# A cross-attention and mixture-of-experts kernel: four groups of expert tiles in place of three, two norms moved to VectorE, five result buffers

## The chip, the core and the metric

The kernel runs on one core of one Trainium2 chip. The metric is the device time of one execution in microseconds (us). Engines are called PE (TensorE), DVE (VectorE), ACT (ScalarE), POOL (GpSimd) and SP (SyncE, which here only issues DMAs). Each engine works through its own list of instructions in order; they meet at semaphores.

## What is computed

Two layers over 8 batches of 256 tokens of width 128. The part that the change touches is the end of the second layer:

```python
x = x + tanh(g_xattn[1]) * xattn(layernorm(x), ctx)      # 16 heads of width 8, softmax
z = layernorm(x)                                         # the fourth norm, per batch of 256 tokens
gates = z @ gate_w + gate_b                              # 8 experts
scores, idx = top_k(gates, 2); g = softmax(scores)
for each expert e: h = gelu(z @ w1[e] + b1[e]); y[e] = h @ w2[e] + b2[e]
x = x + tanh(g_ffn[1]) * (sum of the two chosen y, weighted by g)
```

Tokens, weights and results of this part are fp32.

## The kernel before, in words

**Tiles.** Every token is written twice, once for each chosen expert, into a DRAM table `sorted_rows`, at a row that groups the tokens by expert (`sort_rows(b)`: four indirect DMAs from GpSimd for each batch b). The expert layer then runs over NT = 23 tiles of 256 rows; each tile belongs to one expert. For tile n SP loads the expert's weights (`load_weights(n)`, 4 buffers) and the 256 rows (`load_rows(n)`, 4 buffers); PE transposes the rows (`turn_tokens`), DVE copies them out of the accumulation bank (`take_tokens`), PE makes the hidden layer (`hidden`), ACT the GELU (`gelu_tile`), PE the result (`output`), DVE adds the bias into a result buffer (`weigh`, buffer n % 3) and GpSimd scatters it (`scatter`, two indirect DMAs). At the end all results are read back and added.

**Groups.** Which expert a tile has depends on how many tokens chose each expert, so tiles are planned in groups (`PHASES`): after batch 5 the first 5 tiles are certain to be full, after batch 6 two more, and after batch 7 the remaining 16. `begin_tiles(phase)` is that planning: a chain of 17 small DVE instructions, each waiting for the one before it. It ends by setting the tile's expert and place, which SP reads into a register before it issues a load.

**Slots.** The attention over batch n is `step_c(n)`, written out as 18 slots, k = 0 to 17, and every engine runs its own list for each slot. In step n the attention of batch n runs beside the scores of batch n + 1 (`m`) and the end of batch n - 1 (`o`): softmax sums are turned, inverted and spread (slots 2 to 5), the heads are scaled (`on`, slot 4), multiplied by We (slot 8), added to x (slot 8, line 1222), its variance is taken (slots 10, 11), GpSimd makes the reciprocal deviation (`rstd_of`, lines 496 and 499) and the norm (`fourth_norm`, lines 585 to 594), PE turns the normed tokens (slot 16, line 1700). The gates of batch n - 2 are made in slot 0, its two experts picked (`top_two`, `choose`), and its rows placed (`find_place`, slot 13, line 1291).

Step 8 is the tail: no attention is left in it, only the end of batch 7, the gates and places of batch 6, and the first tiles. PE's list there is: gates of batch 6 (slot 0), turn the sums (2), rank the choices of batch 6 (3), spread the inverted sums (5), We (8), then tile 0 and tile 1 (`turn_tokens(0)`, `hidden(0)`, `turn_tokens(1)`, `hidden(1)`, slot 10), then the normed tokens of batch 7 (16). DVE takes the tokens of tiles 0 and 1 in slot 12 and then runs `begin_tiles(1)`. SP issues the first weight load only when all attention is done (`attended`), because weight and row buffers lie on memory that attention uses, and the first row load when batches 0 to 5 are sorted. GpSimd's list in step 8 is: norm of batch 7, then `sort_rows(6)`.

After step 8 a loop over n runs `hidden(n + 1)`, `turn_tokens(n + 2)`, `output(n)` on PE and `take_tokens(n + 2)`, `weigh(n)` on DVE; the gates, choice and place of batch 7 and `begin_tiles(2)` sit inside the first two passes.

Of the kernel before, what the change touches and what calls it, by code (L numbers as in the profile page):

```python
# [16 lines left out]
U32 = mybir.dt.uint32  # L17
# [5 lines left out]
P = 128  # L23
# [20 lines left out]
PHASES = ((0, 5), (5, 2), (7, NT - 7))  # L44
KNOWN = (BATCH - 3, BATCH - 2, BATCH - 1)
# [84 lines left out]
def flamingo(nc, t):  # L130
    ctx = ExitStack()
    with ctx:
# [150 lines left out]
        nmax = [sb(f"nmax{i}", [P, 2, 2, 2, QUADS], scope=c) for i in range(2)]  # L283
        c.close()
# [4 lines left out]
        soft = sb("soft", [P, 4, TILES], scope=d)  # L289
        weight = sb("weight", [P, TILES, 2], scope=d)  # L290
        spare = [sb(f"spare{i}", [P, 2], scope=d) for i in range(2)]
        to_row = [sb(f"to_row{i}", [P, 2], U32, d) for i in range(4)]
        wbuf = [sb(f"wbuf{i}", [P, PACK], scope=d) for i in range(WB)]
        xg = [sb(f"xg{i}", [P, 2, ROW], scope=d) for i in range(4)]
        xg_t = [sb(f"xg_t{i}", [P, SLOT], scope=d) for i in range(2)]
        hid = [sb(f"hid{i}", [P, HC, SLOT], scope=d) for i in range(2)]
        yout = [sb(f"yout{i}", [P, SLOT], scope=d) for i in range(3)]
# [42 lines left out]
        def _(sp):  # L340
# [117 lines left out]
            for i in range(3):  # L458
                sp.wait_ge(sem(f"y_out{i}"), 32 * ((NT - 1 - i) // 3 + 1))
# [15 lines left out]
        def _(pool):  # L475
# [104 lines left out]


# [61 lines left out]
            for n in range(1, BATCH + 1):  # L643
                if n + 1 < BATCH:
                    widen_v(Step(0, n + 1, BATCH))
                if 2 <= n < BATCH:
                    choose(pool, n - 2)
                fourth_norm(Step(0, n - 1, BATCH))
                if n >= 2:
                    sort_rows(n - 2)  # L650

            def scatter(n):
# [3 lines left out]
                for i in range(2):  # L656
                    pool.indirect_dma_start(  # L657
                        out=y_rows[:, :], out_offset=bass.IndirectOffsetOnAxis(ap=to_row[n % 4][:, i:i + 1], axis=0),
                        in_=yout[n % 3][:, i * P:(i + 1) * P], in_offset=None)\
                        .then_inc(sem(f"y_out{n % 3}"), 16)  # L660
# [1135 lines left out]
```

## Time and profile before

| what | value |
|---|---|
| median of 3 runs | 412.39 us (411.47 to 415.35) |
| profiled execution, own time | 412.65 us |
| its span in the profile | 410.9 us |
| PE busy | 307.9 us (75%) |
| DVE busy | 265.3 us (65%) |
| ACT busy | 198.1 us (48%) |
| POOL busy | 162.6 us (40%) |

The span is what the trace shows of that execution; 1.75 us of its time lie outside it. All times below are microseconds from the start of the span. The attention steps run until about 280, step 8 and the first tiles from 280 to 311, the rest of the tiles until 384, and the final sums until the end. Busy time is an average over stages with different limits, so what counts is the stage in which a change lies.

### The profile page before, as it was taken

What the parts mean: (1) busy time and instruction counts of PE and PEld (TensorE: products, weight loads), DVE (VectorE), ACT (ScalarE), POOL (GpSimd) and SP (SyncE); (2) the same over time, 40 slices, a digit from 0 to 9 for tenths busy, and PEclk for the clock granted to TensorE, in tenths of its full rate; (3) what the DMA queues carried; (4) which work ended last, traced back from release to release, by engine and by line L of the source; (5) the groups of instructions that cost most, each with busy time, mean ns of one, the idle gap of its engine ahead of it and who ended that gap; (6) DMA issues with size and microseconds to landing.
All of it is one profiled execution on the core that took longest, in us unless ns stands there. A gap on an engine that the chain in (4) does not pass through costs nothing.

```text
span 410.9 us, 7400 instructions
## 1 busy us (share of the span) xinstructions
PE 307.9 (75%) x2316; PEld 250.3 (61%) x2317; DVE 265.3 (65%) x878; ACT 198.1 (48%) x395; POOL 162.6 (40%) x289
## 2 busy tenths in 40 slices
PE   1568785271476999999999999995498999999300
PEld 0457774210333787877877787664398999999300
DVE  4647887498983978978979797855274323232162
ACT  1136664454923667666566666563153544454100
POOL 4350111450552401215272644633627644554432
PEclk9959999575557799999999999998699999999855
DMA  7434672554010111101110111005536878874171
GB/s 196 150 128 180 241 274 46 69 86 109 1 38 2 24 32 24 25 22 46 37 46 21 49 27 40 21 8 172 178 101 203 259 227 246 233 219 137 47 247 51
DMA packets 30618, 43.76 MB, mean 106 GB/s; under 512 B 5075, under 2 KB 24086, under 8 KB 30198
## 3 DMA queue, kind: packets, MB, share of 16 engines
q1 hardware_dynamic: 25798, 35.71, 30.1%
q0 software_dynamic: 3008, 6.23, 4.8%
q10 hardware_dynamic: 1776, 1.38, 1.1%
q8 instruction: 18, 0.29, 0.3%
q14 instruction: 18, 0.15, 0.1%
HBM read 21.99 MB, written 15.01 MB: 90 GB/s over the span
## 4 chain that ended last, share of the span: by engine, by line
PE 63%; DVE 11%; DMA 8%; issue 7%; POOL 6%; ACT 2%; DVEq 0%; SPq 0%; POOLq 0%
PE bank L1419 57%; DMA k_all<-k_hi 3%; DVE x L1390 2%; POOL k_all L315 2%; DVE nmax L1172 1%; PE bank L1734 1%; DMA xg<-sorted_rows 1%; DMA y_in<-y_rows 1%; DVE xn L919 1%; DMA sorted_rows<-token_row,place 1%; PE bank L1667 1%; POOL x L547 1%; PE bank L1445 1%; DMA x<-in_x 1%; PE bank L1679 1%
## 5 line engine op out<-in xcount | busy, mean ns | idle before, releaser
L837 ACT ACTIVATE probs<-bank 128x512 f32<-128x512 f32 x128 | 71.0, 597 | 43.9 <-PE bank L1419 43.7
L1172 DVE TENSOR_REDUCE nmax<-bank 128x2 f32<-128x512 f32 x128 | 81.7, 678 | 4.4 <-PE bank L1419 3.7
L848 ACT ACTIVATE hid<-bank,wbuf 128x256 f32<-128x256 f32 x92 | 39.6, 475 | 52.7 <-PE bank L1419 52.7
L657 POOL DMA_INDIRECT y_rows<-yout,to_row x46 | 44.0, 957 | 39.3 <-DVE yout L1379 31.4
L1419 PE MATMUL bank<-q_st,k_quad 128*128 128x256 f32 x256 | 56.0, 308 | 0.8 <-ACT probs L837 0.7
L1419 PE MATMUL bank<-k_quad,q_st 128*128 128x256 f32 x256 | 53.7, 296 | 1.6 <-ACT q_st L800 0.7
L1419 PE MATMUL bank<-xg_t,wbuf 128*128 128x256 f32 x184 | 45.3, 390 | 2.4 <-issue 1.8
L1419 PEld LDWEIGHTS bank<-q_st,k_quad 128*128 128x128 f32 x256 | 38.7, 193 | 11.9 <-ACT probs L837 11.2
L1419 PE MATMUL bank<-wbuf,hid 128*128 128x128 f32 x368 | 45.0, 275 | 0.5 <-DVE yout L1379 0.5
L1419 PEld LDWEIGHTS bank<-wbuf,hid 128*128 128x128 f32 x368 | 43.0, 192 | 0.8 <-DVE yout L1379 0.7
L1419 PEld LDWEIGHTS bank<-k_quad,q_st 128*128 128x128 f32 x256 | 40.5, 196 | 3.9 <-DVE nmax L1172 2.2
L496 POOL TENSOR_TENSOR var_eps<-mv,eps_row 128x2 f32<-128x2 f32 (+1 forms) x20 | 4.0, 201 | 90.2 <-DVE mv L934 87.4
L1419 PEld LDWEIGHTS bank<-xg_t,wbuf 128*128 128x128 f32 x184 | 34.2, 196 | 7.0 <-issue 3.1
L606 POOL DMA_INDIRECT sorted_rows<-token_row,place x32 | 31.7, 991 | 11.1 <-issue 8.6
L1419 PE MATMUL bank<-probs,v_st 128*32 128x256 f32 x512 | 34.3, 385 | 0.7 <-ACT probs L837 0.7
L1363 DVE COPY xg_t<-bank 128x256 f32<-128x256 f32 x23 | 9.8, 424 | 32.9 <-PE bank L1734 32.8
L1379 DVE TENSOR_TENSOR yout<-bank,wbuf 128x256 f32<-128x256 f32 x23 | 9.7, 424 | 20.2 <-PE bank L1419 20.2
L1419 PEld LDWEIGHTS bank<-probs,v_st 128*32 128x32 f32 x512 | 13.4, 109 | 10.6 <-ACT probs L837 1.0
L1445 PE MATMUL bank<-ident,ctx_in 128*128 128x128 f32 x16 | 3.9, 331 | 20.7 <-DVE xn L946 12.2
L575 POOL TENSOR_TENSOR v_st<-v,bv 128x64 f32<-128x64 f32 x32 | 9.2, 323 | 23.0 <-PE bank L1419 22.8
L1192 DVE TENSOR_TENSOR q_st<-bank,q_st 128x512 fp32r<-128x512 f32 x16 | 11.0, 685 | 9.8 <-PE bank L1419 9.8
L499 POOL TENSOR_TENSOR rstd<-var_eps,half_neg 128x2 f32<-128x2 f32 (+1 forms) x20 | 15.8, 788 | 1.6
(237 smaller groups left out, 589.4 us busy)
## 6 DMA issues: line engine op xcount, KB each, us to landing
wbuf<-in_moe_pack SPq DMA_DIRECT2D x23, 578.0 KB, 4.1
sorted_rows<-zeros SPq DMA_DIRECT2D x15, 572.0 KB, 4.1
k_quad<-k_all SPq DMA_DIRECT2D x64, 48.0 KB
xg<-sorted_rows SPq DMA_DIRECT2D x23, 132.0 KB, 3.5
ctx_in<-in_ctx SPq DMA_DIRECT2D x8, 128.0 KB, 2.8
x<-in_x SPq DMA_DIRECT2D x4, 256.0 KB, 5.1
k_all<-k_hi SPq DMA_DIRECT2D x16, 64.0 KB
k_all<-k_lo SPq DMA_DIRECT2D x16, 64.0 KB
```

The source lines that it names most:

```text
L315: eng.dma_start(k_all[32 * j + 8 * s:32 * j + 8 * s + 8, g, :].bitcast(F32), src[r0:r0 + 8, :].bitcast(F32)).then_inc(sem(f"k_slotted{s // ...
L499: pool.tensor_tensor(out[:, 0:tiles], eps_sum[:, 0:tiles], half_neg[:, 0:tiles], ALU.pow)\
L575: pool.tensor_tensor(dst[:, :, :, 48 * r:48 * r + 8], heads(v1f[:, ds(s.n * SEQ + i * P, P)]), heads(bv1[:, :]), ALU.add)\
L606: pool.indirect_dma_start(out=sorted_rows[:, :], out_offset=bass.IndirectOffsetOnAxis(ap=place[:, c:c + 1], axis=0), in_=token_row[b % 3][ ...
L657: pool.indirect_dma_start(out=y_rows[:, :], out_offset=bass.IndirectOffsetOnAxis(ap=to_row[n % 4][:, i:i + 1], axis=0), in_=yout[n % 3][:, ...
L837: act.activation(probs[quad % 2][:, j, :, :], bank[2 + j % 2][:, :] .rearrange("p (r s) -> p r s", r=2), ACT.Exp, scale=SC1)\
L848: act.activation(hid[n % 2][:, ch, :], bank[ch][:, 0:SLOT], ACT.Gelu, bias=wbuf[n % WB][:, B1P + ch:B1P + ch + 1]).then_inc(sem("gelued"), 1)
L1172: dve.tensor_reduce(nmax[m.par][:, gp, qt, :, j], bank[QUERY_BANKS[u % 3]][:, :].rearrange("p (r s) -> p r s", r=2), AX.X, ALU.max, negate ...
L1192: dve.tensor_tensor(qs, bank[5][:, :].rearrange("p (g s) -> p g s", g=2), qs.bitcast(F32), ALU.add).then_inc(sem("q_shifted"), 1)
L1363: dve.tensor_copy(xg_t[n % 2][:, :], bank[6][:, 0:SLOT]).then_inc(sem("xg_t_ready"), 1)
L1379: dve.tensor_tensor(yout[n % 3][:, :].rearrange("p (i d) -> p i d", d=DM), bank[5][:, 0:SLOT].rearrange("p (i d) -> p i d", d=DM), wbuf[n ...
L1419: return pe.matmul(out, lhsT, rhs, start=start, stop=stop, **kw)
```

## The change

- The groups are now (0, 3), (3, 2), (5, 2), (7, 16): the first three tiles are planned after batch 4, in step 7 slot 6, the next two after batch 5 (step 7 slot 14), two more after batch 6 (step 8 slot 12).
- Weight and row buffers, scatter indices and shares are moved to memory that attention does not use; SP no longer waits for `attended`.
- PE's list in step 8: gates of batch 6 (slot 0, another bank), `turn_tokens(0)` (1), sums (2), ranks of batch 6 (3), `hidden(0)` and `turn_tokens(1)` (4), spread (5), We (8), `hidden(1)`, `turn_tokens(2)` and `output(0)` (10), normed tokens of batch 7 (16).
- DVE's list in step 8: gates and choice of batch 6 (0), reciprocal (1), `take_tokens(0)` (2), `on` (4), place of batch 6 (5), x (8), variance and the new `late_norm(7)` (10, 11), then `take_tokens(1)`, `take_tokens(2)`, `weigh(0)` and `begin_tiles(2)` (12).
- The norms of batches 6 and 7 are made by DVE (`late_norm`, four instructions), GpSimd only makes the reciprocal deviation. In step 8 GpSimd runs `sort_rows(6)` first and that of batch 7 second.
- Five result buffers in place of three, seven sets of scatter indices in place of four.

```diff
+YB = 5
+PHASES = ((0, 3), (3, 2), (5, 2), (7, NT - 7))
+KNOWN = (BATCH - 4, BATCH - 3, BATCH - 2, BATCH - 1)
...
-            sp.wait_ge(sem("attended"), 4 * BATCH)
+            first = PHASES[1][0]
             sp.wait_ge(sem("tiles_set"), 2)
-            for n in range(WB):
+            for n in range(first):
                 load_weights(n)
-            for i in range(2):
-                sp.wait_ge(sem(f"rows_sorted{i}"), 64 * 3)
-            for n in range(4):
+            sp.wait_ge(sem("rows_sorted0"), 64 * 3)
+            sp.wait_ge(sem("rows_sorted1"), 64 * 2)
+            for n in range(first):
                 load_rows(n)
-            for n in range(4, NT):
+            for n in range(first, NT):
                 if n == PHASES[1][0]:
                     sp.wait_ge(sem("tiles_set"), 4)
-                    sp.wait_ge(sem("rows_sorted2"), 64)
+                    sp.wait_ge(sem("rows_sorted1"), 64 * 3)
                 if n == PHASES[2][0]:
                     sp.wait_ge(sem("tiles_set"), 6)
+                    sp.wait_ge(sem("rows_sorted2"), 64)
+                if n == PHASES[3][0]:
+                    sp.wait_ge(sem("tiles_set"), 8)
...
+                if b.n >= BATCH - 2:
+                    pool.wait_ge(sem(f"rows_sorted{(b.n - 3) % 2}"), 64 * ((b.n - 3) // 2 + 1))
+                    pool.tensor_copy(token_row[b.n % 3][:, :, :, DM], row_no[:, 2 * b.n:2 * b.n + 2, :])\
+                        .then_inc(sem("rows_named"), 1)
+                    rstd_of(b.n + (LN4 + 1), mv[b.par], var_eps[b.par], rstd[b.par], 2)
+                    return
...
-                pool.wait_ge(sem("rows_named"), 2 * b + 2)
+                late = max(0, b - (BATCH - 3))
+                pool.wait_ge(sem("rows_named"), 2 * b + 2 - late)
+                if late:
+                    pool.wait_ge(sem("xn4_copied"), late)
...
+                if n == BATCH:
+                    sort_rows(n - 2)
                 fourth_norm(Step(0, n - 1, BATCH))
-                if n >= 2:
+                if 2 <= n < BATCH:
...
+                    if is_step(s, BATCH) and k == 5:
+                        gelu_tile(0)
                     if is_step(s, BATCH) and k == 15:
-                        gelu_tile(0)
+                        gelu_tile(1)
...
+                        if is_step(o, BATCH - 2) or is_step(o, BATCH - 1):
+                            late_norm(o.n)
...
+                    if is_step(s, BATCH - 1) and k == 6:
+                        begin_tiles(0)
                     if is_step(s, BATCH - 1) and k == 14:
-                        begin_tiles(0)
+                        begin_tiles(1)
+                    if is_step(s, BATCH) and k == 2:
+                        take_tokens(0)
                     if is_step(s, BATCH) and k == 12:
-                        take_tokens(0)
                         take_tokens(1)
-                        begin_tiles(1)
+                        take_tokens(2)
+                        weigh(0)
+                        begin_tiles(2)
                     if m.valid and k == 9:
                         split_maxima(m, 0)
                     if m.valid and k == 13:
                         shift_q(m, 0)
                     if m.valid and 0 <= k - QUERY_LAG < 16:
                         maximum(k - QUERY_LAG)
+
+            def late_norm(b):
+
+                late = b - (BATCH - 3)
+                dve.wait_ge(sem("rstd_done"), b + (LN4 + 1))
+                dve.wait_ge(sem("rows_named"), 2 * b + 2 - late)
+                for k, ready in ((0, "xn4_ready"), (1, "xn4_copied")):
+                    for i in range(2):
+                        ins = norm(token_row[b % 3][:, i, k, 0:DM], x[:, b * SEQ + i * P:b * SEQ + (i + 1) * P], b % 2, i)
+                    ins.then_inc(sem(ready), 1)
...
-                if n >= 3:
-                    dve.wait_ge(sem(f"y_out{n % 3}"), 32 * (n // 3))
-                dve.tensor_tensor(yout[n % 3][:, :].rearrange("p (i d) -> p i d", d=DM),
+                if n >= YB:
+                    dve.wait_ge(sem(f"y_out{n % YB}"), 32 * (n // YB))
...
-            for n in range(NT):
+            add_gate_bias(BATCH - 1, bank[4][:, 0:16])
+            top_two(BATCH - 1)
+            choose(dve, BATCH - 1)
+            dve.tensor_tensor(soft[:, 0, :], top[:, :, 1], top[:, :, 0], ALU.subtract).then_inc(sem("top_gap"), 1)
+            for n in range(1, NT):
                 if n + 2 < NT:
                     take_tokens(n + 2)
                 weigh(n)
-                if n == 0:
-                    add_gate_bias(BATCH - 1, bank[4][:, 0:16])
-                    top_two(BATCH - 1)
-                    choose(dve, BATCH - 1)
-                    dve.tensor_tensor(soft[:, 0, :], top[:, :, 1], top[:, :, 0], ALU.subtract).then_inc(sem("top_gap"), 1)
                 if n == 1:
                     find_place(BATCH - 1, bank[4][:, 16:40])
-                    begin_tiles(2)
+                    begin_tiles(3)
...
+                        pe.wait_ge(sem("q_shifted"), 2 * BATCH)
+                        project_gates(BATCH - 2, bank[5][:, 0:16])
+                    if is_step(s, BATCH) and k == 1:
                         pe.wait_ge(sem("s_maxed"), 16 * BATCH)
-                        project_gates(BATCH - 2, bank[0][:, 0:16])
+                        turn_tokens(0)
                     if is_step(s, BATCH) and k == 3:
-                        rank_choices(BATCH - 2, bank[1])
+                        pe.wait_ge(sem("gates_ready"), BATCH - 1)
+                        rank_choices(BATCH - 2, bank[5][:, 16:40])
+                    if is_step(s, BATCH) and k == 4:
+                        pe.wait_ge(sem("exped"), 16 * BATCH)
+                        hidden(0)
+                        turn_tokens(1)
                     if s.valid and s.n >= 2 and k == 11:
                         pe.wait_ge(sem("x3_done"), o.n + 1)
                         rank_choices(s.n - 2, bank[7])
                     if is_step(s, BATCH) and k == 10:
+                        hidden(1)
+                        turn_tokens(2)
                         pe.wait_ge(sem("rank_step"), 3 * (BATCH - 2) + 2)
-                        pe.wait_ge(sem("counted"), 2)
-                        pe.wait_ge(sem("exped"), 16 * BATCH)
-                        pe.wait_ge(sem("q_shifted"), 2 * BATCH)
-                        turn_tokens(0)
-                        hidden(0)
-                        turn_tokens(1)
-                        hidden(1)
+                        pe.wait_ge(sem("counted"), 3)
+                        output(0)
...
-                if n and n + 1 < NT:
+            for n in range(1, NT):
+                if n + 1 < NT:
                     hidden(n + 1)
+                if n == 1:
+                    project_gates(BATCH - 1, bank[4][:, 0:16])
                 if n + 2 < NT:
                     turn_tokens(n + 2)
                 output(n)
-                if n == 0:
-                    project_gates(BATCH - 1, bank[4][:, 0:16])
                 if n == 1:
                     rank_choices(BATCH - 1, bank[4][:, 16:40])
```

## Rows read from the trace of the kernel before

**Rows 1.** Stretches: PE, PEld, DVE, ACT, POOL busy us (count); granted clock; DMA share
```profile
285.00:286.00 1.00, 0.77 (x5) 0.77 (x6) 0.71 (x6) 0.24 (x2) 0.00 (x0) 0.78 0.98 351
330.00:360.00 30.00, 30.00 (x210) 27.95 (x209) 8.61 (x32) 13.86 (x33) 15.31 (x16) 1.00 0.78 233
```

**Rows 2.** The chain of work that ended last: start, length, what
```profile
286.64 4.96 DMA xg<-sorted_rows
...
310.58 1.97 PE bank L1419 x8
```

**Rows 3.** Timeline of DVE, step 7: start, length, engine, line, operation, out<-in, count
```profile
270.01 0.69 DVE L1216 TENSOR_TENSOR on<-av,bank 128x512 f32<-128x512 f32 x1 [0.75 <-PE bank L1679]
...
272.90 0.48 DVE L1222 SCALAR_TENSOR_TENSOR x<-bank,tg,x 128x256 f32<-128x256 f32 x1 [2.21 <-PE bank L1419]
...
275.81 0.22 DVE L1316 TENSOR_SCALAR whole<-count 128x8 f32<-128x8 f32 x1
...
279.90 0.16 DVE L1355 TENSOR_TENSOR used<-base,ends 128x8 f32<-128x8 f32 x1
```

**Rows 4.** First weight loads (timeline, SP), and landing of row loads (line 434)
```profile
281.26 3.76 SPq L425 DMA_DIRECT2D wbuf<-in_moe_pack  x4
...
DMA to landing us min/median/max: 2.9/3.5/5.0
```

**Rows 5.** Timeline of DVE and PE in step 8
```profile
280.85 0.17 DVE L1250 TENSOR_TENSOR gates<-bank,gate_b 128x16 f32<-128x16 f32 x1 [0.80 <-PE bank L1419]
...
282.72 0.35 DVE L1210 RECIPROCAL sums_inv<-bank 128x32 f32<-128x32 f32 x1
...
283.79 0.66 PE L1679 MATMUL bank<-ident,inv_wide 128*128 128x128 f32 x4 [0.75 <-ACT inv_wide L812]
284.49 0.69 DVE L1216 TENSOR_TENSOR on<-av,bank 128x512 f32<-128x512 f32 x1 [1.41 <-PE bank L1679]
...
285.59 0.16 DVE L1291 SCALAR_TENSOR_TENSOR place<-top_f,rank 128x4 uint32<-128x4 f32 x1
```

**Rows 6.** Timeline of GpSimd: end of batch 7, then the sort of batch 6
```profile
288.44 0.19 POOL L496 TENSOR_TENSOR var_eps<-mv,eps_row 128x2 f32<-128x2 f32 x1 [6.25 <-DVE mv L934]
288.71 0.73 POOL L499 TENSOR_TENSOR rstd<-var_eps,half_neg 128x2 f32<-128x2 f32 x1
...
291.49 1.08 POOL L606 DMA_INDIRECT sorted_rows<-token_row,place  x1 [0.18 <-issue]
...
295.39 0.95 POOL L606 DMA_INDIRECT sorted_rows<-token_row,place  x1 [0.30 <-issue]
```

**Rows 7.** Timeline of DVE: four norms of 128x128 in the third norm
```profile
112.61 1.10 DVE L919 TENSOR_SCALAR xn<-x,mv,rstd 128x128 f32<-128x128 f32 x4
```

**Rows 8.** Timeline of PE: hidden(0), hidden(1), output(0)
```profile
293.00 3.34 PE L1419 MATMUL bank<-xg_t,wbuf 128*128 128x256 f32 x8 [0.61 <-DVE xg_t L1363]
...
297.13 1.97 PE L1419 MATMUL bank<-xg_t,wbuf 128*128 128x256 f32 x8 [0.56 <-issue]
...
299.37 1.95 PE L1419 MATMUL bank<-wbuf,hid 128*128 128x128 f32 x16
```

**Rows 9.** Timeline of DVE among the first tiles
```profile
297.21 0.17 DVE L1316 TENSOR_SCALAR whole<-count 128x8 f32<-128x8 f32 x1
...
300.12 0.16 DVE L1355 TENSOR_TENSOR used<-base,ends 128x8 f32<-128x8 f32 x1
...
301.35 0.42 DVE L1379 TENSOR_TENSOR yout<-bank,wbuf 128x256 f32<-128x256 f32 x1 [0.35 <-PE bank L1419]
...
306.45 0.17 DVE L1316 TENSOR_SCALAR whole<-count 128x8 f32<-128x8 f32 x1
...
310.05 0.42 DVE L1363 COPY xg_t<-bank 128x256 f32<-128x256 f32 x1
```

**Rows 10.** Result buffers (yout): who waited for their instructions (us, times)
```profile
  DVE to_row L1370: 7.8, 8
...
  PE bank L1419: 0.5, 1
```

More of the change, by code:

```diff
@@ L283, in flamingo @@
         nmax = [sb(f"nmax{i}", [P, 2, 2, 2, QUADS], scope=c) for i in range(2)]
+        soft = sb("soft", [P, 4, TILES], scope=c)
+        weight = sb("weight", [P, TILES, 2], scope=c)
+        spare = [sb(f"spare{i}", [P, 2], scope=c) for i in range(2)]
+        to_row = [sb(f"to_row{i}", [P, 2], U32, c) for i in range(YB + 2)]
+        wbuf = [sb(f"wbuf{i}", [P, PACK], scope=c) for i in range(WB)]
+        xg = [sb(f"xg{i}", [P, 2, ROW], scope=c) for i in range(4)]
         c.close()
@@ L288, in flamingo @@
         d = ctx
[L289 to L294, printed above, removed]
         xg_t = [sb(f"xg_t{i}", [P, SLOT], scope=d) for i in range(2)]
         hid = [sb(f"hid{i}", [P, HC, SLOT], scope=d) for i in range(2)]
-        yout = [sb(f"yout{i}", [P, SLOT], scope=d) for i in range(3)]
+        yout = [sb(f"yout{i}", [P, SLOT], scope=d) for i in range(YB)]
         y_in = [sb(f"y_in{i}", [P, BT, 2, DM], scope=d) for i in range(NBLK)]
@@ L456, in load_sums @@
                 sp.dma_start(y_in[k][:, :, :, :], y_tiles[:, BT * k:BT * k + BT, :, :]).then_inc(sem(f"y_landed{k}"), 16)
-            for i in range(3):
-                sp.wait_ge(sem(f"y_out{i}"), 32 * ((NT - 1 - i) // 3 + 1))
+            for i in range(YB):
+                sp.wait_ge(sem(f"y_out{i}"), 32 * ((NT - 1 - i) // YB + 1))
             load_sums(0)
@@ L657, in scatter @@
                     pool.indirect_dma_start(
-                        out=y_rows[:, :], out_offset=bass.IndirectOffsetOnAxis(ap=to_row[n % 4][:, i:i + 1], axis=0),
-                        in_=yout[n % 3][:, i * P:(i + 1) * P], in_offset=None)\
-                        .then_inc(sem(f"y_out{n % 3}"), 16)
+                        out=y_rows[:, :], out_offset=bass.IndirectOffsetOnAxis(ap=to_row[n % (YB + 2)][:, i:i + 1], axis=0),
+                        in_=yout[n % YB][:, i * P:(i + 1) * P], in_offset=None)\
+                        .then_inc(sem(f"y_out{n % YB}"), 16)
             for n in range(NT):
@@ L669, in add_last @@
                 k = NBLK - 1
-                pool.wait_ge(sem("v_step"), 49)
+                pool.wait_ge(sem("v_step"), 64)
                 pool.wait_ge(sem(f"y_landed{k}"), 16)
@@ L851, in _ @@
             unrolled(step_c, BATCH)
-            for n in range(1, NT):
+            for n in range(2, NT):
                 gelu_tile(n)
@@ L858, in load_sums @@
                 act.dma_start(y_in[k][:, :, :, :], y_tiles[:, BT * k:BT * k + BT, :, :]).then_inc(sem(f"y_landed{k}"), 16)
-            for i in range(3):
-                act.wait_ge(sem(f"y_out{i}"), 32 * ((NT - 1 - i) // 3 + 1))
+            for i in range(YB):
+                act.wait_ge(sem(f"y_out{i}"), 32 * ((NT - 1 - i) // YB + 1))
             load_sums(1)
@@ L1315, in begin_tiles @@
                 dve.wait_ge(sem("moe_set"), MOE_SET)
-                dve.tensor_scalar(whole[:, 0, :], count[:, phase, :], exact if phase == 2 else -exact, 1.0 / SLOT,
+                dve.tensor_scalar(whole[:, 0, :], count[:, phase, :], exact if phase == len(PHASES) - 1 else -exact, 1.0 / SLOT,
                                   ALU.add, ALU.mult).then_inc(sem("v_step"), 1)
@@ L1366, in take_tokens @@
                    .then_inc(sem("named"), 1)
-                if n >= 4:
-                    dve.wait_ge(sem(f"y_out{(n - 4) % 3}"), 32 * ((n - 4) // 3 + 1))
+                if n >= YB + 2:
+                    dve.wait_ge(sem(f"y_out{(n - YB - 2) % YB}"), 32 * ((n - YB - 2) // YB + 1))
                 dve.wait_ge(sem("named"), 2 * n + 1)
-                dve.scalar_tensor_tensor(to_row[n % 4][:, :], names, -1.0, spare[n % 2][:, :], ALU.add, ALU.add)\
+                dve.scalar_tensor_tensor(to_row[n % (YB + 2)][:, :], names, -1.0, spare[n % 2][:, :], ALU.add, ALU.add)\
                    .then_inc(sem("named"), 1)
@@ L1757, in _ @@
             unrolled(step_c, BATCH)
-            for n in range(NT):
-                if n and n + 1 < NT:
+            for n in range(1, NT):
+                if n + 1 < NT:
                     hidden(n + 1)
+                if n == 1:
+                    project_gates(BATCH - 1, bank[4][:, 0:16])
                 if n + 2 < NT:
```

19 lines of the change are left out of this document (9 added, 10 removed).

## The prediction, made before the changed kernel was run

> **What bounds the kernel now.** I read the chain of work that ended last first, then the stretches by engine, then the timeline around the end of attention. Late in the run PE is busy 30.00 of 30.00 us and its weight loads 27.95 [rows 1]: PE sets the pace there (210 matmuls in 30 us, 26 a tile: some 3.7 us a tile), and nothing that other engines do in that stretch shortens it. The chain says where that stretch begins: hidden(4) starts at 310.58 [rows 2] and from there on it is matmuls to the last tile. So the question for any change ahead of it is when hidden(4) starts. Its reason is on DVE: the copy for tile 4 is taken at 310.05, right after the planning of the last group, which began at 306.45 [rows 9].
>
> Between attention and hidden(4) there is a gap that the change aims at. SP issues its first weights at 281.26 [rows 4], the first rows follow at 286.64 and take 4.96 us [rows 2], and PE starts hidden(0) only at 293.00 [rows 8]. Meanwhile the end of batch 7 runs through DVE and PE [rows 5], then GpSimd makes its norm and sorts batch 6 [rows 6].
>
> **The change, part by part.**
>
> *Planning and loading earlier.* DVE reaches slot 6 of step 7 when `on` ends at 270.70 and waits there until 272.90 [rows 3], so 2.2 us of the planning of the first group are covered. A planning with few tiles takes 297.21 to 300.28, 3.07 us [rows 9]; the same list beside GpSimd's norm took 275.81 to 280.06, 4.25 us [rows 3]. GpSimd has no norm at that moment now, so I take 3.07: done at 273.8, and x of batch 6 is 1.1 us late. SP's first weight load came 1.2 us after the end of the planning that it needs (280.06 to 281.26), four issues take 3.76 us, some 1.1 each [rows 3, 4]. Three weight loads then go out from 275.0 and the first rows at 278.4. Their landing takes 2.9 to 5.0 us [rows 4]; nearest is the load of before that also queued behind fresh weights, 4.96 [rows 2]. Rows of tile 0 land at 283.4, at 281.3 by the lower bound.
>
> *DVE in step 7* also gets the norms of batch 6: four norms take 1.10 us [rows 7], behind a wait of 1.0 us for the reciprocal deviation (288.44 to 289.44) [rows 6]. With x 1.1 late, place of batch 5 and the second planning move back by 2.7 us and the latter ends near 281.6. The gates of batch 6, taken at 280.85 before [rows 5], start some 0.8 late; with 1.9 us from gates to reciprocal (280.85 to 282.72) [rows 5], the reciprocal can't start before 283.5. That is covered by the rows of tile 0, which are later still. Attention itself is not touched: PE needs the place of batch 5 only in slot 16.
>
> *Tile 0 inside the tail.* PE's list is in order, so turn_tokens(0) holds it until 283.4. Four transposes take 0.66 us [rows 5], two half that: sums turned at 284.5, reciprocal 0.35 [rows 5] and copy 0.42 [rows 9] with their handoffs: hidden(0) starts at 285.6, 7.4 us earlier than the 293.00 of before. So the front does what it is built for. But the granted clock fell in the stretch 285 to 286 (mean 0.78) after PE had been mostly waiting [rows 1], and hidden(0) took 3.34 us against 1.97 for hidden(1) [rows 8], the difference between the levels of 1.2 and 2.4 GHz. PE waits as much here, so I take 3.34. It then turns tile 1 (0.35) and only after that spreads the inverted sums of batch 7 (0.66): `on` starts at 290.1 in place of 284.49 [rows 5]. This is the price: **the end of batch 7 and the place of batch 6 both stand behind tile 0 in PE's list, 5.6 us late.**
>
> *The new order on GpSimd.* Place of batch 6 is 1.26 us after `on` (284.49 to 285.75) [rows 5]: 291.4. GpSimd now runs sort_rows(6) before the reciprocal deviation of batch 7. Four indirect DMAs take 291.49 to 296.34, 4.85 us [rows 6], so from 291.7 to 296.5; with the row names and 1.0 us for the deviation [rows 6] it is there at 297.7. Before, it was there at 289.44, and the norm on GpSimd took from there to the sort at 291.49, about 1.9 us [rows 6]; DVE's 1.10 saves 0.8 of that, on a path that has become 8 us longer.
>
> *What is queued behind the wait.* DVE waits for that deviation in slot 11 with everything behind it: take_tokens(1), take_tokens(2), weigh(0), begin_tiles(2). PE waits for take_tokens(1) with hidden(1), output(0) and the turn of batch 7. Norms until 298.9, copy 0.42 [rows 9], hidden(1) at 299.5 against 297.13 [rows 8]: **2.4 us later than before, though hidden(0) was 7.4 earlier.** PE has then stood still since We, near 291.5, so I price hidden(1) at the lower clock, 3.34. The Trainium skill (TensorE: Matmul & The Clock Gate, section HAM oscillation) says the same of a PE that waits for data between short bursts: each burst begins at the lower clock. By that rule the sum is the one given here, without it 2.7 us less; the two levels in rows 8 agree with it, but no row of before shows this gap.
>
> *From hidden(1) to hidden(4).* hidden(1) 3.34, turn 0.35, output(0) 1.95 [rows 8]: weigh(0) at 305.25, before 301.35 [rows 9], 3.9 later. Then DVE's list is longer than before by a planning, which stood beside tile 1 there (297.21) and stands behind weigh(0) now: weigh 0.42, planning 3.07, gates and choice of batch 7 2.1, tokens of tile 3 0.7, weigh(1) 0.4, place 0.6, last planning 3.6 (306.45 to 310.05) [rows 5, 9]. take_tokens(4) at 316.15 and hidden(4) 0.53 later, as before (310.05 to 310.58), at 316.7 [rows 2, 9]: **6.1 us late.** PE's own work of three tiles fits inside that. GpSimd's sort of batch 7 and the loads of tile 7 follow the same place and planning, and keep their distance to hidden(7).
>
> *Buffers.* DVE waited 7.8 us in 8 waits for scatters before it could write indices; PE waited 0.5 us in all for result buffers [rows 10]. PE covers the former, so five buffers and seven sets are worth 0 to 0.5; I take 0. If the cover were gone they could give 7.8. Moving buffers in memory costs no instruction.
>
> Sum, on the profiled execution (412.65, of which 410.9 are the span): 412.65 + 6.1 = 418.75. It is 0.26 above the median of the runs, so **418.5** is predicted. Bounds: rows landing in 2.9 us gain only 1.2 (the reciprocal's 283.5 then rules), both hidden layers at the upper clock gain 2.7: 414.6. Two plannings on the path at 4.25 in place of 3.07 cost 2.4: 421.
>
> **The rivals.**
> - *A shorter hold-up.* Either the clock stays up (-2.7: 415.8), or GpSimd's sort does not hold the deviation, whose spans are rough in the profile: the deviation then starts 3.95 us after `on` (284.49 to 288.44) [rows 5, 6], at 294.0 in place of 296.7, again 415.8. For it: PE is not quite idle ahead of hidden(0). Against it: the sort's four spans follow each other at 1.3 us, and before, too, hidden(0) came cold after a wait. 0.15.
> - *The other side: the buffers pay.* If the waits of 7.8 us for scatters [rows 10] lie on PE's path after all, hidden behind modelled ends of matmuls, taking them away gives 418.5 - 7.8 = 410.7, not slower. It decides from 6.1 of the 7.8 on. Against it: 30.00 of 30.00 [rows 1] and 0.5 us [rows 10]. 0.07.
> - *The front keeps its gain.* If tile 1 did not wait for the norm of batch 7, hidden(0)'s 7.4 us would move all that follows: 405. Against it stand the written order of DVE's list and of GpSimd's. 0.07.
> - *The loads come no earlier.* If rows of tile 0 land at 291.6 as before, turn_tokens(0) holds PE and the whole tail by 8.2 us more: 426.7. Against it: the planning needs only batch 4. 0.05.
>
> **How the numbers follow.** The forecast has 0.66, its own range is 414.6 to 421.5. The range 410 to 422.5 takes in the shorter hold-up and the buffers and leaves out the front's gain, the late loads and a little of each edge, under 2 in 10. A measurement of this kernel can tell about 1% from no change, so the borders are 408.3 and 416.5. Slower: most of the forecast (0.58), the late loads and some of the shorter hold-up, 0.67. Same: the rest of these two and most of the buffers' case, 0.23. Faster: 0.10.
>
> **What would show it.** Rows of tile 0 in by 283 to 284 and hidden(0) near 285.6 show the front right; a PE gap of some 7 us between We and hidden(1), with DVE waiting for line 499 in it and GpSimd in four indirect DMAs ahead of line 499, shows the hold-up; hidden(1) at 3.3 us shows the clock; hidden(4) near 316.7 shows the sum. I am wrong if hidden(1) starts before 297, or if tiles late in the run take less than 3.7 us.

## The result, and the profile after

The changed kernel takes 419.56 us (median of 20 runs, 416.39 to 421.94) against 413.27 us for the kernel before beside it (20 runs, 410.51 to 416.43): ratio 1.0149, 95% interval 1.0123 to 1.0176. It is slower, by some 6.2 us by the ratio. 418.5 was forecast. The profiled execution has a span of 419.0 us, against 410.9.

Two executions are compared here from one landmark, since they part long before the change. PE's last product for the gates of batch 6 (slot 0 of step 8, the end of attention) stands at 280.13 in the kernel before and at 281.61 after. Timeline of PE, the kernel before, then after: start, length, engine, line, operation, out<-in, size, count, idle time before it and its releaser.

```profile
128.50 1.13 PE L1419 MATMUL bank<-silu,wq 128*128 128x512 f32 x2 [0.69 <-ACT silu L788]
...
280.13 0.61 PE L1419 MATMUL bank<-gate_w,xt 128*128 128x8 f32 x4
...
291.73 0.66 PE L1734 MATMUL bank<-ident,xg 128*128 128x128 f32 x2 [4.71 <-DMA xg<-sorted_rows]
```
```profile
128.46 2.07 PE L1452 MATMUL bank<-silu,wq 128*128 128x512 f32 x2 [0.69 <-ACT silu L803]
...
281.61 0.61 PE L1452 MATMUL bank<-gate_w,xt 128*128 128x8 f32 x4
```

The two products at 128.5 are the same code and took 1.13 us in one execution and 2.07 in the other; the granted clock from 128 to 130 was 0.86 and 0.50, and its mean from 100 to 140 was 0.63 and 0.52. What PE does from here to the landmark is the same work, and other executions of the changed kernel's code up to there reach the landmark anywhere from 277.73 to 281.72 (see the last section). So the 1.48 us, of the 8.1 between the spans, is put down to PE's clock in the two executions and not to the change. From the landmark, call it G, the change is read. Chain of waits that ended last, after (start, length, what):

```profile
275.15 0.48 SPq L423
...
279.61 5.20 DMA xg<-sorted_rows
284.95 0.41 PE bank L1772 x2
...
286.74 3.75 PE bank L1452 x8
290.50 0.43 PE bank L1772 x2
290.92 0.87 PE bank L1717 x4
291.81 0.70 DVE on L1233
292.56 1.16 PE bank L1452 x8
293.71 7.13 issue
300.84 3.75 PE bank L1452 x8
...
317.28 1.15 issue
318.43 1.96 PE bank L1452 x8
```

The rows of tile 0 land 8.3 us earlier than before, counted from G (turn_tokens(0) at G + 3.34, before G + 11.60). hidden(0) starts at 286.74 and takes 3.75 us; its eight products take 1.97 at the upper clock [rows 8]. Then We ends at 293.7, and PE stands for 7.13 us ahead of hidden(1) at 300.84. hidden(4), where the stretch paced by PE begins [rows 1, 2], is at 318.43: G + 36.82 against G + 30.45. That is 6.37 us, and from hidden(4) to the end of the span both take the same, 100.6 and 100.3 us.

What DVE and GpSimd did in the gap of 7.13 us (timelines, after):

```profile
291.81 0.69 DVE L1233 TENSOR_TENSOR on<-av,bank 128x512 f32<-128x512 f32 x1 [4.96 <-PE bank L1717]
...
292.92 0.16 DVE L1325 SCALAR_TENSOR_TENSOR place<-top_f,rank 128x4 uint32<-128x4 f32 x1
...
294.90 0.15 DVE L951 BATCH_NORM_AGGREGATE mv<-stats 128x2 f32<-128x6 f32 x1
299.29 1.12 DVE L936 TENSOR_SCALAR token_row<-x,mv,rstd 128x128 f32<-128x128 f32 x4 [4.24 <-POOL rstd L503]
300.32 0.42 DVE L1397 COPY xg_t<-bank 128x256 f32<-128x256 f32 x1
```
```profile
293.36 0.96 POOL L619 DMA_INDIRECT sorted_rows<-token_row,place  x1 [8.91 <-DVE place L1325]
...
297.14 0.96 POOL L619 DMA_INDIRECT sorted_rows<-token_row,place  x1 [0.30 <-issue]
298.10 0.21 POOL L587 COPY token_row<-row_no 128x4 f32<-128x4 f32 x1
298.25 0.20 POOL L500 TENSOR_TENSOR var_eps<-mv,eps_row 128x2 f32<-128x2 f32 x1
298.53 0.72 POOL L503 TENSOR_TENSOR rstd<-var_eps,half_neg 128x2 f32<-128x2 f32 x1
```

GpSimd had waited 8.91 us for the place of batch 6 and began its four scatters at 293.36. The variance of batch 7 was ready at 295.05, in the middle of them, and GpSimd reached it only at 298.25. DVE waited 4.24 us for the result, and take_tokens(1), for which PE waited, stood behind DVE's norms.

The granted clock in that time (stretches of 2 us: busy us and count of PE, PEld, DVE, ACT, POOL; granted clock; DMA share; GB/s):

```profile
294.00:296.00 2.00, 0.00 (x0) 0.00 (x0) 0.96 (x7) 0.00 (x0) 1.39 (x3) 0.94 0.10 34
296.00:298.00 2.00, 0.00 (x0) 0.00 (x0) 0.00 (x0) 0.00 (x0) 1.70 (x2) 0.50 0.20 68
...
302.00:304.00 2.00, 2.00 (x7) 1.55 (x6) 0.00 (x0) 1.17 (x3) 0.00 (x0) 0.50 0.04 8
304.00:306.00 2.00, 2.00 (x10) 1.80 (x9) 0.65 (x3) 0.73 (x2) 0.00 (x0) 0.50 0.00 0
306.00:308.00 2.00, 2.00 (x17) 1.95 (x17) 0.59 (x3) 0.38 (x1) 0.00 (x0) 1.00 0.00 0
```

It falls to 0.50 (1.2 GHz) while PE stands, and is still there until 306, so hidden(1) takes 3.75 us.

### The profile page after: what moved, and what is told of

The parts are those of the page before. It is cut to its first block, busy times and chain, and to the rows that moved or that the text cites. A ratio compares the mean times of both kernels' runs of the same rounds, so it can differ in the third digit from the quotient of the medians.

```text
span 419.0 us, 7426 instructions
## 1 busy us (share of the span) xinstructions
PE 311.3 (74%) x2317; PEld 252.4 (60%) x2318; DVE 267.3 (64%) x904; ACT 198.4 (47%) x395; POOL 158.9 (38%) x283
## 4 chain that ended last, share of the span: by engine, by line
PE 60%; DVE 11%; issue 11%; DMA 7%; POOL 5%; ACT 2%; SPq 1%; DVEq 0%; POOLq 0%; ACTq 0%
PE bank L1452 54%; DMA k_all<-k_hi 3%; DVE nmax L1189 2%; POOL k_all L316 2%; DMA y_in<-y_rows 2%; PE bank L1772 1%; DMA xg<-sorted_rows 1%; PE bank L1705 1%; DVE xn L936 1%; PE bank L1717 1%; PE bank L1478 1%; POOL x L551 1%; DMA x<-in_x 1%; POOL y_in L690 1%; DVE h L1103 1%
## 5 line engine op out<-in xcount | busy, mean ns | idle before, releaser
L1452 PE MATMUL bank<-xg_t,wbuf 128*128 128x256 f32 x184 | 47.4, 404 | 9.3 <-issue 8.6
L1452 PEld LDWEIGHTS bank<-xg_t,wbuf 128*128 128x128 f32 x184 | 35.4, 203 | 14.1 <-issue 9.8
```

What stands on the lines that cost most here:

```text
L1452: return pe.matmul(out, lhsT, rhs, start=start, stop=stop, **kw)
```

## The experiments

Every kernel below is the changed kernel with the edit shown, and its ratio is to the kernel before on the same chip. The times from G are from the profiled execution of each; from hidden(4) to the end of the span all take 100.3 to 100.9 us, so the fifth column carries the difference. Among eight of these executions whose code is the same up to hidden(0) (after, e1 to e4b, e6 and e7), hidden(0) starts between G + 5.06 and G + 5.91. So differences of less than about 0.9 us in one column tell nothing by themselves.

| kernel | tile 0 turned | hidden(1) | weigh(0) | hidden(4) | ratio (95% interval) |
|---|---|---|---|---|---|
| before | G+11.60 | G+17.00 | G+21.22 | G+30.45 | 1 |
| after | 3.34 | 19.23 | 25.77 | 36.82 | 1.0149 (1.0123 to 1.0176) |
| e1_rstd_first | 3.50 | 16.03 | 21.70 | 33.02 | 1.0062 (1.0027 to 1.0096) |
| e2_take1_early | 3.39 | 12.74 | 19.23 | 30.31 | 0.9967 (0.9937 to 0.9996) |
| e3_three_buffers | 3.58 | 20.00 | 26.77 | 37.85 | 1.0107 (1.0061 to 1.0154) |
| e4_warm | 3.41 | 22.01 | 25.94 | 37.02 | 1.0137 (1.0092 to 1.0182) |
| e4b_warm14 | 3.71 | 19.98 | 23.91 | 34.97 | 1.0070 (1.0028 to 1.0111) |
| e5_loads_late | 9.68 | 25.35 | 31.16 | 42.22 | 1.0238 (1.0182 to 1.0293) |
| e6_place_early | 3.55 | 16.40 | 22.71 | 33.77 | 1.0045 (1.0002 to 1.0089) |
| e9_pool_norms | 3.73 | 13.75 | 17.76 | 29.75 | 1.0013 (0.9974 to 1.0052) |
| e7_all | 3.38 | 13.45 | 18.31 | 28.22 | 0.9898 (0.9838 to 0.9959) |
| e8_front | 4.19 | 10.87 | 14.88 | 24.79 | 0.9849 (0.9797 to 0.9902) |

**The scatter ahead of the last reciprocal deviation.** GpSimd makes rstd(7) first:

```diff
-                if n == BATCH:
-                    sort_rows(n - 2)
                 fourth_norm(Step(0, n - 1, BATCH))
-                if 2 <= n < BATCH:
+                if n >= 2:
```

> Changed kernel, but in step 8 GpSimd makes the reciprocal deviation of batch 7 ahead of sort_rows(6), as before the change. Theory (DVE waits for the deviation behind the sort, and tile 1 behind DVE): the variance of batch 7 is there at 295.05 in the changed kernel's trace, so the deviation comes at 296.1 in place of 299.25 and hidden(1) starts about 3.0 us earlier, near 297.8; all that follows moves with it: about 416.5 where the changed kernel has 419.56. Rival (the sort does not hold the deviation): no change. Rival (buffers or the late part rule): no change.

GpSimd in the timeline of e1_rstd_first now waits for the variance and makes the deviation ahead of the scatters:

```profile
291.19 0.19 POOL L500 TENSOR_TENSOR var_eps<-mv,eps_row 128x2 f32<-128x2 f32 x1 [10.39 <-DVE mv L949]
291.45 0.72 POOL L503 TENSOR_TENSOR rstd<-var_eps,half_neg 128x2 f32<-128x2 f32 x1
292.37 1.11 POOL L619 DMA_INDIRECT sorted_rows<-token_row,place  x1 [0.20 <-issue]
```

Measured 417.29 us; hidden(4) at G + 33.02, 3.8 us earlier than in the changed kernel; hidden(1) is 3.2 earlier and weigh(0) 4.1. The hold-up by the scatters is real and is more than half of the loss.

**The tokens behind the norm.** DVE takes the tokens of tile 1 before it waits for rstd(7):

```diff
                         find_place(BATCH - 2, bank[5][:, 16:40])
+                        take_tokens(1)
...
-                        take_tokens(1)
```

> Changed kernel, but DVE takes the tokens of tile 1 right after the place of batch 6, ahead of x and of the norm of batch 7. Theory: hidden(1) no longer stands behind the norm and starts when We is done, near 293.9, at the upper clock (1.97 in place of 3.75 us); take_tokens(2) and weigh(0) still stand behind the norm, so weigh(0) comes near 301.1 in place of 307.38: about 6 us gained, 413.4. Rival (the end hangs on batch 7's norm alone and not on tile 1): at most 1 us gained.

Measured 413.13 us. PE and DVE in the timelines of e2_take1_early:

```profile
291.04 2.08 PE L1452 MATMUL bank<-we_pad,on 128*128 128x128 f32 x8 [0.78 <-DVE on L1233]
292.91 2.83 PE L1452 MATMUL bank<-xg_t,wbuf 128*128 128x256 f32 x8
...
297.77 1.12 DVE L936 TENSOR_SCALAR token_row<-x,mv,rstd 128x128 f32<-128x128 f32 x4 [3.32 <-POOL rstd L503]
```

hidden(1) follows We at once (G + 12.74; it takes 2.83 us where 1.97 were expected), and the whole loss is gone, though GpSimd's order is that of the change and DVE still waits 3.3 us for rstd(7).

**The result buffers.** `YB = 3` in place of 5 (with it five sets of indices in place of seven):

> Changed kernel with three result buffers and five sets of scatter indices. Theory (PE covers the waits for scatters): no change, 419.6, within 0.5 us; DVE waits for scatters again, some 8 us in all. Rival (the buffers pay up to 7.8 us and hide a larger loss elsewhere): up to 427.

Measured 418.74 us. The interval of the ratio (1.0061 to 1.0154) takes in the changed kernel's 1.0149 and is far from a loss of 7.8 us against it. hidden(4) is 1.03 us later, but 0.78 of that is there at hidden(0), ahead of the first result buffer, and from hidden(4) to the end it is 100.43 us against 100.57. Five buffers are worth nothing that can be seen. DVE's wait of some 8 us for scatters, which was expected back, did not come: with five sets of indices, one more than the kernel before has, DVE never waits for one. So this run tests the buffers, and seven sets against five, but not the four sets of before; those 7.8 us of waits [rows 10] cost the kernel before nothing that shows, as it takes 100.3 us from hidden(4) to the end and the changed kernel 100.6.

**The clock.** PE is kept busy ahead of hidden(1) with products whose results nobody reads:

```diff
                     if is_step(s, BATCH) and k == 10:
+                        for _ in range(24):
+                            mm(bank[4][:, 0:SLOT], ident[:, :], causal[:, 0:SLOT])
                         hidden(1)
```

> Changed kernel with 24 extra products of 128x256 on PE between We and hidden(1), into a bank that nobody reads; they add nothing to the result and fill some 5.8 of the 7.1 us in which PE waits. Theory: hidden(1) starts at the same time but at the upper clock, 1.97 in place of 3.75 us, with the turn and output(0) behind it some 0.8 us shorter: 2.6 us gained in all, 417.0. Rival (the clock is no part of the loss, the path goes through DVE alone): no change.

Measured 420.12 us: no gain. The 24 products were mis-sized: 5.8 us was expected for them. Each is two matmuls in the trace, together they took 10.53 us, and hidden(1) came 2.8 us late (G + 22.01). But from hidden(1) to weigh(0) it took 3.93 us in place of 6.54. So the same with `range(14)`:

> The changed kernel with 14 products whose results nobody reads, put on TensorE between the gates' products of batch 7 (L1720's part We) and hidden(1). The run with 24 of them showed 0.434 us for one (10.53 us for 24), so 14 take about 6.1 us, from some 293.7 to 299.8 in the changed kernel's frame, and end ahead of hidden(1)'s data (300.84). Theory (the low clock behind the idle stretch adds 1.8 us to hidden(1) and 0.6 us to output(0)): hidden(1) starts where it did, its 8 products take 1.9 to 2.0 us in place of 3.75, the step from hidden(1) to weigh(0) takes 3.9 us in place of 6.54, and the time is 2.6 us less than the changed kernel's: ratio 1.0085 to the kernel before. Rival (VectorE's planning of group 2 behind weigh(0), not TensorE's clock, sets hidden(4)): weigh(0) earlier, hidden(4) and the time where they were, ratio 1.014.

Measured 416.9 us. Timeline of PE in e4b_warm14:

```profile
291.53 2.08 PE L1452 MATMUL bank<-we_pad,on 128*128 128x128 f32 x8 [0.78 <-DVE on L1233]
293.40 7.08 PE L1452 MATMUL bank<-causal,ident 128*128 128x256 f32 x28
300.32 1.89 PE L1452 MATMUL bank<-xg_t,wbuf 128*128 128x256 f32 x8
```

The 14 products took 7.08 us where 6.1 were expected, so hidden(1) is still 0.75 us later than in the changed kernel (0.37 of it is there when tile 0 is turned). Yet it takes 1.89 us, and from hidden(1) to hidden(4) it is 14.99 us in place of 17.59: 2.60 less. Useless work buys back 1.85 us net. The second part of the loss is the clock, a consequence of the gap. The granted clock of e4b_warm14 there:

```profile
296.00:298.00 2.00, 2.00 (x11) 1.76 (x10) 0.00 (x0) 0.00 (x0) 1.80 (x4) 1.00 0.20 68
```

**The loads.** SP waits for the end of attention again before its first weights:

```diff
+            sp.wait_ge(sem("attended"), 4 * BATCH)
             first = PHASES[1][0]
```

> The changed kernel with SyncE waiting, ahead of the first loads of the experts' weights, for the end of attention, as the kernel before did. Theory (the early loads are worth what they save in turn_tokens(0)): the weights are issued at about 282.7 in place of 276.15, the rows of group 0 land at about 291, hidden(0) comes some 6.2 us later than in the changed kernel and everything behind it by as much, less what planning group 2 and the place of batch 6 no longer cost because VectorE does them inside the wait: between 3 and 6.2 us more, ratio 1.022 to 1.030. Rival (the loads are hidden anyway, the hold-up by GpSimd's scatters and VectorE's late norms is the whole loss): hidden(1) and hidden(4) stay where they are, ratio 1.015.

Measured 423.02 us. Tile 0 is turned 6.3 us later, and hidden(4) is 5.40 us later. The chain of waits in e5_loads_late shows why hardly anything of it was covered:

```profile
282.33 4.95 DMA xg<-sorted_rows
...
295.96 7.13 issue
303.09 3.75 PE bank L1453 x8
```

The hold-up ahead of hidden(1) is 7.13 us here too: it hangs on `on` and the place of batch 6, which stand behind tile 0 in PE's list, and moves with it. The early loads do gain; the gain is smaller than what the new order loses.

**The place of batch 6.** It is found right behind take_tokens(0), ahead of the wait for the spread:

```diff
-                    if is_step(s, BATCH) and k == 5:
-                        find_place(BATCH - 2, bank[5][:, 16:40])
...
                     if is_step(s, BATCH) and k == 2:
                         take_tokens(0)
+                        find_place(BATCH - 2, bank[5][:, 16:40])
```

> The changed kernel with one piece of VectorE's order moved: the place of batch 6 is found right behind take_tokens(0), ahead of the gates' addition that waits for TensorE's spread, in place of behind it. Theory (the scatter of batch 6 holds up GpSimd's last rstd because the place comes late): the four scatters run from about 288 to 292.8, ahead of the last variance (295.05) rather than across it; rstd(7) follows the variance at once, the late norms start at about 296 in place of 299.3, hidden(1) at 297.5 in place of 300.84, and the time is 3 us less than the changed kernel's: ratio 1.007, as with the rstd made first. Rival (the hold-up is the scatters' own cost to VectorE or to the DMA queues, wherever they stand): no change, ratio 1.014.

Measured 416.31 us; hidden(4) 3.05 us earlier. The scatters run from 287.97 to 292.72, and GpSimd then waits 2.46 us for the variance. That agrees with e1_rstd_first by another way: scatters out of the road of rstd(7), before it or after it, give 3 to 4 us.

**The norms.** GpSimd makes them as before, with the change's order of its list (that is, the scatters first):

```diff
-                if b.n >= BATCH - 2:
...
-                    return
...
-                late = max(0, b - (BATCH - 3))
+                late = 0
...
-                        if is_step(o, BATCH - 2) or is_step(o, BATCH - 1):
-                            late_norm(o.n)
```

> The changed kernel with one part undone: GpSimd makes the norms of batches 6 and 7 again, as in the kernel before; loads, groups, planning and buffers are those of the change, and GpSimd still sends batch 6's rows out (293.36 to 298.10) ahead of its last rstd. Theory (the loss comes from putting VectorE's norms, which wait for that rstd, ahead of take_tokens(1) in VectorE's order): VectorE has no wait of 4.2 us any more, take_tokens(1) follows the last variance (295.05 in the changed kernel's frame), hidden(1) starts at about 295.6 in place of 300.84 and hidden(4) some 5.2 us earlier; GpSimd's norm is ready at about 300.6 (rstd to 299.25, then 0.60, 0.18 and half of 1.17 us as in the kernel before), in time for TensorE's turn behind output(0). The time is 5.2 us less than the changed kernel's: ratio 1.002. Rival (GpSimd's slower norms hold up the gates of batch 7 by as much as VectorE's did hidden(1)): ratio 1.012 or more.

Measured 413.39 us, no different from the kernel before. PE, DVE and GpSimd in the timelines of e9_pool_norms:

```profile
295.15 0.39 DVE L1389 COPY xg_t<-bank 128x256 f32<-128x256 f32 x1
...
295.64 1.97 PE L1444 MATMUL bank<-xg_t,wbuf 128*128 128x256 f32 x8 [1.74 <-issue]
...
300.68 0.44 PE L1730 MATMUL bank<-ident,token_row 128*128 128x128 f32 x2 [1.07 <-POOL token_row L598]
```
```profile
297.33 0.96 POOL L613 DMA_INDIRECT sorted_rows<-token_row,place  x1 [0.30 <-issue]
298.31 0.21 POOL L500 TENSOR_TENSOR var_eps<-mv,eps_row 128x2 f32<-128x2 f32 x1
298.60 0.73 POOL L503 TENSOR_TENSOR rstd<-var_eps,half_neg 128x2 f32<-128x2 f32 x1
```

GpSimd's deviation is as late as ever, and its norm is slower. Nobody but the turn of batch 7 waits for it, and that waits 1.07 us, behind output(0). PE's gap shrinks to 1.74 us and hidden(1) runs at the upper clock, so hidden(4) comes 7.07 us earlier: 5.48 by hidden(1), 2.53 between hidden(1) and weigh(0), and 0.94 lost again behind weigh(0). 5.2 were expected, without the clock.

**Both orders mended, and a faster kernel.** First DVE's list alone:

```diff
-                    if is_step(s, BATCH) and k == 5:
-                        find_place(BATCH - 2, bank[5][:, 16:40])
...
+                        if is_step(o, BATCH - 1):
+                            take_tokens(2)
                         if is_step(o, BATCH - 2) or is_step(o, BATCH - 1):
                             late_norm(o.n)
...
                     if is_step(s, BATCH) and k == 2:
                         take_tokens(0)
+                        find_place(BATCH - 2, bank[5][:, 16:40])
+                        begin_tiles(2)
+                    if is_step(s, BATCH) and k == 5:
+                        take_tokens(1)
                     if is_step(s, BATCH) and k == 12:
-                        take_tokens(1)
-                        take_tokens(2)
                         weigh(0)
-                        begin_tiles(2)
```

> The changed kernel with VectorE's order rearranged throughout step 8: the place of batch 6 and the plan of group 2 stand right behind take_tokens(0), where VectorE waited 4.9 us; take_tokens(1) behind the gates' addition; take_tokens(2) between the last variance and the two late norms; weigh(0) after them. Theory (the loss is the order of VectorE's and GpSimd's work round hidden(1), nothing else of the change): hidden(1) follows the gates' products at once (about 293), the late norms come before 298, hidden(4) at about 309 in place of 318.4, and the time is some 9.5 us less than the changed kernel's: about 410 us, ratio 0.992. Rival (another stage behind hidden(4), such as the results' way out, takes over once the front is short): hidden(4) at 309, the time less by under 6 us, ratio 0.998 or more.

Measured 410.44 us, 1.0% below the kernel before. hidden(4) is 8.60 us earlier than in the changed kernel: 5.78 by hidden(1), 1.68 between hidden(1) and weigh(0) (the clock, in part: hidden(1) still takes 2.82), 1.14 behind weigh(0), where the planning of group 2 no longer stands. That planning takes 3.07 us, but behind weigh(0) DVE now waits 1.87 us for the gates of batch 7:

```profile
300.49 0.17 DVE L1285 TENSOR_TENSOR gates<-bank,gate_b 128x16 f32<-128x16 f32 x1 [1.87 <-PE bank L1453]
```

Then PE's and GpSimd's lists too, shown against the changed kernel:

```diff
-                if n == BATCH:
-                    sort_rows(n - 2)
...
-                    if is_step(s, BATCH) and k == 1:
+                    if is_step(s, BATCH) and k == 6:
                         pe.wait_ge(sem("s_maxed"), 16 * BATCH)
                         turn_tokens(0)
...
-                    if is_step(s, BATCH) and k == 4:
+                    if is_step(s, BATCH) and k == 9:
                         pe.wait_ge(sem("exped"), 16 * BATCH)
                         hidden(0)
```

In DVE's list `take_tokens(0)` stands in slot 5 here, `find_place` behind the variance, and `take_tokens(1)`, `begin_tiles(2)`, `take_tokens(2)` ahead of weigh(0) in slot 12. So it differs from e7_all in all three lists: the place of batch 6 and the planning of group 2 are later than there.

> The rearranged kernel of the run before (e7_all), with two more moves: TensorE does the sums and the spread of batch 7 while it waits for group 0's rows, and the gates' products ahead of hidden(0), as the kernel before did; GpSimd makes rstd(7) ahead of batch 6's scatters, and VectorE finds batch 6's place behind the last variance and plans group 2 behind take_tokens(1). Theory (what is left ahead of hidden(4) is the order of work in step 8): from the last gates' product of attention to hidden(4) 25.5 us in place of 28.2 in e7_all and 36.8 in the changed kernel, the gates' addition 5 us earlier, hidden(1) 2 to 3 us earlier, the time 2 to 3 us less than e7_all's: ratio 0.983. Rival (the later scatter of batch 6 and the later plan make group 2's rows land after TensorE is ready for them, or TensorE's low clock takes the gain back): hidden(4) where e7_all has it, ratio 0.990.

Measured 407.98 us, 1.5% below the kernel before. Timeline of PE in e8_front:

```profile
281.60 0.66 PE L1703 MATMUL bank<-ident,av 128*128 128x128 f32 x4 [0.18 <-ACT av L820]
...
284.51 0.66 PE L1715 MATMUL bank<-ident,inv_wide 128*128 128x128 f32 x4 [0.75 <-ACT inv_wide L825]
285.00 0.38 PE L1770 MATMUL bank<-ident,xg 128*128 128x128 f32 x2
285.95 1.75 PE L1450 MATMUL bank<-we_pad,on 128*128 128x128 f32 x8 [0.56 <-DVE on L1231]
287.48 3.02 PE L1450 MATMUL bank<-xg_t,wbuf 128*128 128x256 f32 x8
...
291.68 1.97 PE L1450 MATMUL bank<-xg_t,wbuf 128*128 128x256 f32 x8 [0.96 <-issue]
```

The sums now lie in the wait for tile 0's rows, as they lay in the wait for the loads before the change, and the spread stands ahead of tile 0, which then waits for nothing. Tile 0 is turned 0.8 us later than in e7_all, hidden(1) comes 2.6 us earlier and hidden(4) 3.4. That is the worth of the three lists together; no run moves PE's list alone. The profiled spans, 408.6 and 406.0, and G (279.88 and 280.81) agree with that; the two intervals of the ratio overlap, so the step from e7_all to e8_front rests on the trace.

## Why the prediction was right, step by step

Counted in the frame of before (1.48 us taken off the trace of after).

- *The front.* Planning(0) done 273.8 forecast, 273.7 measured; first weights 275.0 and 274.7; rows issued 278.4 and 278.1; landing 4.96 and 5.20; hidden(0) 285.6 and 285.3. Right, also that nothing of attention moved.
- *The price in PE's list.* `on` at 290.1, measured 290.3; place of batch 6 at 291.4, measured 291.6. Right. What it costs alone isn't shown: e8_front, which takes it away, wins 3.4 us over e7_all, but with changes in the lists of DVE and GpSimd.
- *DVE in step 7.* Mis-sized, without effect: the second planning was to end at 281.6 and the gates of batch 6 to start 0.8 late. It ended at 280.8, and the gates started on time.
- *The hold-up.* Scatters 291.7 to 296.5, measured 291.9 to 296.6; rstd at 297.7, measured 297.8; norms until 298.9 and 298.9; hidden(1) at 299.5, measured 299.4, 2.23 us late against G. e1, e2, e6 and e9 each break one link of it. What the prediction didn't see is how little had to be broken: it is the link from DVE's norms to take_tokens(1) that matters most, as e2 gives back all of the loss with the scatters where they were. It priced their move to DVE as 0.8 us saved; the e9 run shows their place in DVE's list as 7.07 us lost.
- *The clock.* Mis-sized. hidden(1) 3.34 was forecast, by hidden(0) of before, and measured 3.75: the clock was low for all of it, and for the turn and most of output(0) behind it. From hidden(1) to weigh(0) 5.75 were forecast, 6.54 measured. The trace agrees with what the prediction weighed from the Trainium skill (TensorE: Matmul & The Clock Gate, section HAM oscillation), that work behind such a wait begins at the lower clock: with PE kept at work the 2.60 us came back.
- *From weigh(0) to hidden(4).* 11.45 forecast, 11.05 measured. The chain of DVE's pieces was priced 0.4 too long, which took back half of the clock's 0.8: that the sum came so close is in part luck. As a sum it held; as a price of the fourth group it did not: with the planning moved, 1.14 us came back and not 3.07, because the gates of batch 7 are then what DVE waits for.
- *Buffers* 0: right within the interval of e3_three_buffers. One reading was wrong: PE's 0.5 us in [rows 10] was no wait for a result buffer, since it is 0.5 us with five buffers as well.

Together, 36.6 forecast for hidden(4) from G (316.7) and 36.82 measured; the time 418.5 and 419.56. Of that difference 0.88 us is the kernel before, which had 412.39 in the forecast and 413.27 beside the measurement. The upper bound of the forecast's own range adds up to 420.9, not 421.5.

The rivals. The shorter hold-up did not come. Of its two halves the deviation free of the scatters was priced well, at 2.7 (3.8 and 3.05 in e1 and e6, with a part of the clock). That the clock's 2.7 meets the 2.60 of e4b_warm14 is luck: the 2.7 were hidden(0) and hidden(1) at the upper clock, while in e4b_warm14 hidden(0) still took 3.75 us, and the 2.60 came from hidden(1) and what follows it. Buffers: refuted. "The front keeps its gain" was 7.4 us below the kernel before. Its condition, that tile 1 does not wait for the norm of batch 7, holds in e2 and e9, and there hidden(4) is only 0.1 and 0.7 us earlier than before: in e2 a lead of 7.8 us at hidden(0) is 4.3 at hidden(1), 2.0 at weigh(0) and 0.1 at hidden(4), as the rest of the new order takes it. So that rival's price was wrong even on its own condition. e8_front, with the order mended, is 5.66 below in the trace. "Loads no earlier" was given 8.2 us more than the forecast; e5_loads_late shows 5.40, since only three weights go ahead of the rows now and they need no planning to wait for.

In timed runs the differences are smaller than in the trace for some kernels (e5: 0.9% of the kernel's time, some 3.7 us, for the 5.40), within their intervals of about 0.5%.

## What to carry to other kernels

When work is moved to a faster engine, look first at what stands behind it in that engine's list: four norms of 1.12 us in all, which wait for another engine, cost 7 us because the tokens of the next tile were queued behind them. When loads are brought forward, the place where the data is consumed should not go ahead of short links of another chain in the consumer's list; put the short links into the wait for the data, as e8_front does. Count the consequence of a gap on PE, too: 7 us of standing cost 2.6 more afterwards.

## What the runs showed of the hardware

The granted clock did not come back with the work: after the gap it was at 0.50 from 296 to 306, through 5 us in which PE was busy all the time. In e4b_warm14, where PE did not stand between We and hidden(1) and had been busy all the time since 291.53, it was at 1.00 from 296 on.

The same code drew different clocks in different executions: G lies between 277.73 (e1_rstd_first) and 281.72 (e4_warm), though neither edit touches what comes before it; the mean granted clock from 100 to 140 was 0.67 in the first and 0.54 in the second. Differences of 1% between single executions of this kernel tell nothing; from a landmark behind that stretch they do, down to the 0.9 us by which hidden(0) varies.

Scatters of GpSimd and small instructions of DVE hardly disturbed each other here. In e7_all the planning of group 2 ran beside the four scatters, in 3.34 us in place of 3.07, and these took 0.96 us each, as anywhere. The Trainium skill (SBUF — State Buffer, section SBUF: two separate sides) warns that a DMA issued from GpSimd is starved of its descriptors while DVE runs an operation in a mode that takes the port both share; no run here shows it, with these small operations. Beside GpSimd's norm of batch 6 and the first scatters behind it the same chain, for five tiles, took 4.25 us [rows 3]; that the norm is the reason is not tested.
